# A two-layer block (selective scan, then experts): scan output and z kept with channels in rows

## The reference, cut to what matters

```python
z = zxbcdt[..., :D_INNER]
dt = softplus(zxbcdt[..., -H_SSM:] + dt_bias)
xBC = silu(causal convolution of 4 taps over the next 768 columns)
Y_diag = einsum('bcln,bcsn,bhcls,bcshp->bclhp', Cr, Br, Lmat, xdt)
Y_off = einsum('bcln,bchpn,bhcl->bclhp', Cr, states_prev, exp(Acs))
y = Y_diag + Y_off + D_param[None, None, :, None] * x_ssm
y = rmsnorm(y * silu(z), norm_gated_w)
out = y @ W_out.T + residual
```

## Time and profile before

| | |
|---|---|
| three executions, median (range) | 3193.36 us (3184.57 to 3193.8) |
| profiled execution, its own time | 3187.6 us |
| its span | 3185.9 us |
| TensorE clock granted, mean | 0.989 |
| busy: PE, PEld, DVE, ACT, POOL | 98%, 85%, 75%, 61%, 64% |

### The profile page before, as it was taken

How to read it: one execution, slowest core, us unless ns; L and a number is a source line. 1 busy time by engine, 2 the same in 40 slices (tenths; PEclk the granted TensorE clock), 3 DMA queues, 4 the chain that set the end, 5 groups by cost and what they waited for, 6 DMA issues and landing times.

```text
span 3185.9 us, 62383 instructions
## 1 busy us (share of the span) xinstructions
PE 3112.3 (98%) x19648; PEld 2722.1 (85%) x19648; DVE 2394.2 (75%) x5104; ACT 1935.2 (61%) x4149; POOL 2031.2 (64%) x2311
## 2 busy tenths in 40 slices
PE   5899999999999999999999999999999999999997
PEld 4688888888888888888888888888888888888886
DVE  5877877777777777777777777778777777777763
ACT  5565666665666556666566666656656656665562
POOL 2477666677666676656676666776666776666764
PEclk7899999999999999999999999999999999999999
DMA  3123222222222222222122222222222222222222
GB/s 123 41 68 87 73 73 67 66 66 85 73 64 64 71 73 76 80 66 58 64 86 76 76 60 66 66 86 73 73 66 66 66 86 73 64 67 69 73 74 48
DMA packets 143433, 227.33 MB, mean 71 GB/s; under 512 B 18976, under 2 KB 88352, under 8 KB 143392
## 3 DMA queue, kind: packets, MB, share of 16 engines
q1 hardware_dynamic: 126496, 210.06, 20.1%
q0 software_dynamic: 16896, 16.78, 4.0%
HBM read 174.87 MB, written 35.13 MB: 66 GB/s over the span
## 4 chain that ended last, share of the span: by engine, by line
PE 95%; DVE 0%; POOL 0%; ACT 0%; issue 0%; ACTq 0%; DVEq 0%; POOLq 0%
PE fpb L1443 34%; PE apb L1443 20%; PE acc L1629 17%; PE apb L1575 7%; PE apb L1452 4%; PE ppb L1443 3%; PE apb L1560 3%; PE apb L1567 2%; PE ppb L1462 2%; PE apb L1547 1%; PE fpb L1492 1%; PE fpb L1462 1%; PE fpb L1494 1%; PE fpb L1608 0%; PE apb L1520 0%; PE apb L1519 0%
## 5 line engine op out<-in xcount | busy, mean ns | idle before, releaser
L652 POOL TENSOR_TENSOR hidL<-hid,hidH 128x512 fp32r<-128x512 f32 x384 | 544.9, 1419 | 234.8 <-ACT hidH L914 226.8
L1130 DVE SCALAR_TENSOR_TENSOR xc<-apb,cw,xc 128x511 f32<-128x511 f32 (+2 forms) x576 | 427.8, 747 | 63.9 <-ACT xc L827 35.9
L1629 PE MATMUL acc<-WDH,hidH 128*128 128x256 f32 x1536 | 456.7, 297 | 4.4 <-POOLq L654 4.4
L914 ACT CAST hidH<-hid 128x512 fp32r<-128x512 f32 x384 | 236.2, 615 | 341.9 <-POOL hid L647 283.6
L1629 PE MATMUL acc<-WDH,hidL 128*128 128x256 f32 x1536 | 431.4, 281 | 0.0
L1629 PE MATMUL acc<-WDL,hidH 128*128 128x256 f32 x1536 | 430.9, 281 | 0.0
L647 POOL TENSOR_TENSOR hid<-hid,cb 128x512 f32<-128x512 f32 x256 | 347.5, 1358 | 73.2 <-DVEq L1251 42.1
L1249 DVE TENSOR_TENSOR hid<-hid,fpb 128x512 f32<-128x512 f32 x384 | 261.1, 680 | 135.6 <-PE fpb L1443 132.3
L1443 PE MATMUL fpb<-fTh,UH 128*128 128x512 f32 x768 | 335.7, 437 | 0.0
L845 ACT ACTIVATE seg<-seg,acs 128x128 f32<-128x128 f32 x1024 | 313.6, 389 | 11.5 <-ACT cb L895 5.7
L1443 PE MATMUL fpb<-fTh,GH 128*128 128x512 f32 x768 | 318.6, 415 | 0.0
(11 more groups left out here) (195 smaller groups left out, 8669.6 us busy)
## 6 DMA issues: line engine op xcount, KB each, us to landing
seg<-acs_row SPq DMA_DIRECT2D x128, 512.0 KB, 4.2
cb<-c_row SPq DMA_DIRECT2D x512, 128.0 KB, 2.9
xsP<-in_x SPq DMA_DIRECT2D x32, 512.0 KB, 3.6
xc<-qrot SPq DMA_DIRECT2D x32, 512.0 KB, 3.4
xc<-in_x SPq DMA_DIRECT2D x32, 512.0 KB, 4.3
out<-xc SPq DMA_DIRECT2D x32, 512.0 KB, 3.0
out<-xn POOLq DMA_DIRECT2D x32, 512.0 KB, 6.0
ZL_loaded<-in_wzx_t SPq DMA_DIRECT2D x2, 512.0 KB, 4.4
```

The costliest lines, as they stand in the source:

```text
L652: own.do(G.tensor_tensor(hidL[:, j % 2, :], hid[:, j % 2, :], hidH[:, j % 2, :].bitcast(fp32), ALU.subtract))
L914: A.copy(hidH[:, j % 2, :], hid[:, j % 2, :]).then_inc(sem["hidden_high"], 1)
L1130: ins = V.scalar_tensor_tensor(xc[:, b, s:], src[:, 0:T - s], cw[:, b, TAPS - 1 - s:TAPS - s], xc[:, b, s:], ALU.mult, ALU.add)
L1629: ins = nc.tensor.matmul(dst, l[:, w, tk], r[:, j, :], start=j == 0 and t % 2 == 0 and n == 0, stop=j == HB - 1 and n == 2, skip_group_che ...
```

## The change

The scan output and z are kept with channels in rows (128 channels x 512 tokens, four such blocks) from the matmul on.

- `project_z(j)` makes one block of z, 128 channels by 512 tokens, four per sequence. dt is computed apart by `project_dt`: 16 narrow matmuls (16 and 8 columns moving) into their own bank, read by `dt_bias_add` in two operations.
- `diagonal` swaps its operands: 64 columns of `xdt` are stationary and the 128 columns of `seg` move. Even heads write PSUM partitions 0 to 63, odd heads 64 to 127, so two heads lie side by side in the array's column halves.
- `from_state` becomes four matmuls with S stationary and C moving. The decay along the row that `state_part` needs is read from DRAM as rows (`own_rows` on SP, two DMAs) and exponentiated in one ACT operation over 128x1536 (`row_exp`) into `own_decay`, which shares its place with xTh and xTl.
- `times_dt` takes the D term from `xc` in SBUF, not from PSUM.
- `y_by_channel` is gone: `evac_y` and `y_low` read `zs` in SBUF.
- The sum of squares now goes over partitions: `square_y` writes the squares, `sum_squares` (DVE, two additions per chunk) folds four blocks to one, `squares_by_token` (PE) multiplies them by a column of ones, `squares_out` copies the result.
- yTh and yTl are guarded by `yT_read` and `out_begun` in place of PSUM slots; all step tables are written anew, in all stages.

```diff
+        own_decay = sb("own_decay", [P, (NT - 1) * NB, P])
...
+                    ("G3", "ACT", "ACT"), ("U2", "DVE", "DVE"), ("U3", "DVE", "DVE"), ("cT", "ACT", "ACT"),
+                    ("G4", "ACT", "ACT"), ("U4", "DVE", "DVE"), ("G5", "ACT", "ACT"), ("U5", "DVE", "DVE"),
...
+                sp.wait_ge(sem["acs_stored"], 16)
+                for a in range(2):
+                    sp.dma_start(own_decay[a * PD:(a + 1) * PD, :, :],
+                                 rows(acs_row, [[0, PD], [2 * P, (NT - 1) * NB], [1, P]], (HS + a) * P)
+                                 ).then_inc(sem["ear_loaded"], 16)
...
-                ins = G.tensor_tensor(zs[:, c, :], zs[:, c, :], xD[:, c % 2, :], ALU.mult)
+                gate = zs[:, :, c * P:(c + 1) * P]
+                ins = G.tensor_tensor(gate, gate, xD[:, c % 2, :].rearrange("p (j n) -> p j n", j=NB), ALU.mult)
...
+            def silu_z(j):
+                way.filled(act, "ACT", f"z{j}")
+                free("a", f"z{j}", A.activation(zs[:, j, :], way.bank(f"z{j}")[:], ACT.Silu))
+
+            def row_exp():
+                act.wait_ge(sem["ear_loaded"], 32)
+                A.activation(own_decay[:], own_decay[:], ACT.Exp).then_inc(sem["ear_ready"], 1)
...
             def evac_y(c):
-                way.filled(act, "ACT", f"yT{c}")
-                A.copy(yTh[:].rearrange("p j n -> p (j n)"), way.bank(f"yT{c}")[:]).then_inc(sem["yh_ready"], 1)
+                act.wait_ge(sem["yg_ready"], c + 1)
+
+                if c == 2:
+                    act.wait_ge(sem["out_begun"], 1)
+                elif c:
+                    act.wait_ge(sem["yT_read"], (c + 1) // 2)
+                A.copy(yTh[:], zs[:, :, c * P:(c + 1) * P]).then_inc(sem["yh_ready"], 1)
...
             def square_y(c):
+                act.wait_ge(sem["yg_ready"], c + 1)
                 if c >= 2:
-                    own.wait()
-                ins = A.activation(junk[c % 2], zs[:, c, :], ACT.Square, accum_out=ssy[:, c:c + 1])
-                if c % 2:
-                    ins.then_inc(sem["ssy_ready"], 1)
-                else:
-                    own.mark(ins)
+                    act.wait_ge(sem["sq_summed"], 1)
+                A.activation(junk[c % 2].rearrange("p (j n) -> p j n", j=NB), zs[:, :, c * P:(c + 1) * P], ACT.Square
...
-            def dt_bias_add(c):
-                way.filled(dve, "DVE", f"za{c}")
-                ins = V.tensor_tensor(dr[:, c, :], way.bank(f"za{c}")[:, DI // 2:DI // 2 + HS], dtb[:], ALU.add)
...
+            def dt_bias_add():
+                way.filled(dve, "DVE", "dt")
+                parts = way.bank("dt")[:, 0:2 * NT * HS].rearrange("p (t a h) -> p t a h", t=NT, a=2)
+                own.do(V.tensor_tensor(dr[:], parts[:, :, 0, :], dtb[:].unsqueeze(1).broadcast_to([P, NT, HS]), ALU.add))
+                own.do(V.tensor_tensor(dr[:], dr[:], parts[:, :, 1, :], ALU.add))
...
-                free("a", f"xt{c}", V.tensor_tensor(by_head(xD[:, c % 2, :]), by_head(way.bank(f"xt{c}")[:]),
-                                                    along(dbc[:]), ALU.mult))
+
+                ins = V.tensor_tensor(by_block(xD[:, c % 2, :]), xc[:, 0:NB, c * P:(c + 1) * P],
+                                      dcol[:].unsqueeze(2).broadcast_to([P, NB, P]), ALU.mult)
...
+            def own_part(c):
+                return own_decay[:, (c - 1) * NB:c * NB, :]
+
             def state_part(c):
                 way.filled(dve, "DVE", f"yo{c}")
-                own.do(V.tensor_tensor(by_head(ysp[:]), by_head(way.bank(f"yo{c}")[:]), along(ea[:, c, :]), ALU.mult))
+                if c == 1:
+                    dve.wait_ge(sem["ear_ready"], 1)
+                own.do(V.tensor_tensor(own_part(c), by_block(way.bank(f"yo{c}")[:]), own_part(c), ALU.mult))
                 free("a", f"yo{c}")
...
+                    ins = V.tensor_tensor(by_block(xdt[:, c % 2, :]), own_part(c), by_block(way.bank(f"yd{c}")[:]), ALU.add)
...
+                if c == 2:
+                    dve.sem_inc(sem["xT_free"], 1)
...
+            def out_begins():
+
+                dve.wait_ge(sem["out_ready"], 1)
+                dve.sem_inc(sem["out_begun"], 1)
...
             def y_low(c):
                 dve.wait_ge(sem["yh_ready"], c + 1)
-                free("a", f"yT{c}", V.tensor_tensor(yTl[:].rearrange("p j n -> p (j n)"), way.bank(f"yT{c}")[:],
-                                                    yTh[:].rearrange("p j n -> p (j n)").bitcast(fp32), ALU.subtract))
+                V.tensor_tensor(yTl[:], zs[:, :, c * P:(c + 1) * P], yTh[:].bitcast(fp32),
...
+            def sum_squares(c):
+
+                dve.wait_ge(sem["sq_ready"], c + 1)
+                q = junk[c % 2]
+                own.do(V.tensor_tensor(q[:, 0:2 * P], q[:, 0:2 * P], q[:, 2 * P:4 * P], ALU.add))
+                V.tensor_tensor(q[:, 0:P], q[:, 0:P], q[:, P:2 * P], ALU.add).then_inc(sem["qs_ready"], 1)
...
+            def squares_out(s):
+                way.filled(dve, "DVE", f"ss{s}")
+                own.do(V.tensor_copy(ssy[:, pair(s)], way.bank(f"ss{s}")[:, 0:2]))
+                free("a", f"ss{s}")
...
-            def project_z(c, n):
-
-                name, tk = f"z{'ab'[n]}{c}", slice(c * P, (c + 1) * P)
...
+            def project_dt():
+                b = slot("dt")
+
+                pe.wait_ge(s_hT, 2)
+                pe.sem_inc(s_hT, -2)
+                fill("dt", narrow(b, hTh, hTl, DTW, HS))
+
+            def project_z(j):
+
+                name, lo = f"z{j}", j * P + (HS if j >= NB // 2 else 0)
+                cs = slice(lo, lo + P)
...
                 read_out(f"st{c - 1}")
-                fill(f"yo{c}", nc.tensor.matmul(b[:], xc[:, 5, c * P:(c + 1) * P], S[:], start=True, stop=True))
+                for j in range(NB):
+                    js = slice(j * P, (j + 1) * P)
+                    ins = nc.tensor.matmul(b[:, js], S[:, js], xc[:, 5, c * P:(c + 1) * P], start=True, stop=True)
+                fill(f"yo{c}", ins)
 
...
-                    hs = slice(h * PD, (h + 1) * PD)
-                    ins = nc.tensor.matmul(b[:, hs], seg[:, c % 2, h, :], xdt[:, c % 2, hs], start=True, stop=True)
+
+                    half = slice(h % 2 * PD, (h % 2 + 1) * PD)
+                    ins = nc.tensor.matmul(b[half, h // 2 * P:(h // 2 + 1) * P], xdt[:, c % 2, h * PD:(h + 1) * PD],
+                                           seg[:, c % 2, h, :], start=True, stop=True)
                 fill(f"yd{c}", ins)
 
-            def y_by_channel(c):
-                b = slot(f"yT{c}")
-                pe.wait_ge(sem["yg_ready"], c + 1)
-                fill(f"yT{c}", transposes(b, lambda j: zs[:, c, j * P:(j + 1) * P], NB))
+            def squares_by_token(s):
+                b = slot(f"ss{s}")
+                for n in range(2):
+                    c = 2 * s + n
+                    pe.wait_ge(sem["qs_ready"], c + 1)
+                    ins = nc.tensor.matmul(b[:, n:n + 1], junk[n][:, 0:P], ones[:, 0:1], start=True, stop=True)
+                fill(f"ss{s}", ins)
...
                 b = way.bank(f"out{s}") if t % 2 else slot(f"out{s}")
-                read_out(f"yT{t}")
-                ins = split_mm(b[:, (t % 2) * D:(t % 2 + 1) * D], [(yTh[:, j, :], yTl[:, j, :], WOH[:, j, :], WOL[:, j, :])
-                                                                   for j in range(NB)])
+                pe.wait_ge(sem["yl_ready"], t + 1)
+                ins = split_mm(b[:, (t % 2) * D:(t % 2 + 1) * D],
+                               [(yTh[:, j, :], yTl[:, j, :], WOH[:, j, :], WOL[:, j, :]) for j in range(NB)])
...
+                h_by_channel(1); gate(11); settled("f_out_ACT"); settled("qn_ready"); up(11)
+                settled("f_out_DVE")
                 assert not open_
 
             def tail():
                 begin("tail", "afg")
...
```

More of the change, by code:

```diff
@@ L88, in build @@
         xdec = sb("xdec", [P, 2, DI])
[L89 removed]
+        xD = sb("xD", [P, 2, DI])
         seg = sb("seg", [P, 2, HS, P])
@@ L1054, in split_low @@
                 dve.wait_ge(s_high[n], 1)
-                for src, hi, lo, norm in SPLIT[n][1]:
+                for m, (src, hi, lo, norm) in enumerate(SPLIT[n][1]):
+                    if m:
+                        own.do(ins)
                     if norm is None:
@@ L1441, in split_mm @@
                 for ah, al, bh, bl in parts:
-                    for l, r in ((ah, bh), (ah, bl), (al, bh)):
+                    for l, r in ((ah, bh), (al, bh), (ah, bl)) if read is not None else ((ah, bh), (ah, bl), (al, bh)):
                         ins = nc.tensor.matmul(dst, l, r, start=n == 0, stop=n == total - 1)
@@ new lines, in iteration @@
+                gate(1); cumulate(); up(1); settled("ad_ready"); project_z(1); gate(2); project_x(3)
+                project_z(2); up(2); project_z(3); gate(3); CB(); B_by_token(); x_by_token(0); down(0)
+                settled("acc_free"); x_by_token(1); up(3); down(1); combine_by_expert(); down(2)
```

(17 more changed lines are left out.)

441 lines of the change are left out of this document (206 added, 235 removed).

## The result

The changed kernel takes 3366.83 us (median of 4 executions, 3363.69 to 3368.86), the kernel before, beside it, 3189.96 (4 executions, 3184.57 to 3193.8): ratio **1.0555 [1.0534, 1.0576]**, slower by 177 us or 5.7 us in each of the 31 passes. I had forecast 3164 and a range up to 3248. Both are wrong, and so is the sign.

What follows compares the result with a forecast made beforehand. TensorE, busy 98% of the span, was taken as the bound: -1.44 us of work and +0.5 of waits give -0.94 us per pass, times 31 = -29 us, so 3164 us; 8-in-10 range 3135 to 3248.

Steps and rivals of the forecast that it cites:

- term 7: Work off TensorE: VectorE rises from 73.9 to 80 to 86 us per pass; ScalarE, SP and POOL cost nothing.
- +0.5 of waits: TensorE's waits per pass, in us, around the output projections: 0.4 at squares_by_token(1), at worst 1.6; bounds 0 and 2.4.
- Everything else I checked: Other places where TensorE might wait, such as project_q(0) and project_out(1): each keeps about 1 us of slack.
- Rival A: VectorE falls behind at squares_by_token(1) and the output projections: 1.4 to 2.4 us of waits, 3192 to 3223 us; chance 0.15.
- Term 6: The diagonal: two column halves run together, 1.00 us plus 0.25 for switching array shape, against 1.73; -1.92 us per pass.
- Rivals B: At the diagonal the two column halves don't run together: +0.30 us per diagonal, 3245 us; chance 0.18.
- C: At the diagonal one half's loads don't hide behind the other's streams: +1.16 us per diagonal, 3352 us; chance 0.03.
- My estimate of 1.6x for two tiles: Alternative for the diagonal, from the skill's 2.38x for three column tiles: 1.1 us in place of 1.00.
- Terms 1 to 5: TensorE, us per pass: z -0.40, dt +1.68, y's transpositions -1.76, from_state +0.09, squares by ones +0.87.
- The sum without waits: TensorE's work per pass changes by -1.44 us, from a pass of 96.40 us.
- Rival D: The clock falls for one projection group after the pass's narrow matmuls and transpositions: +1.4 us per pass, 3208 us; chance 0.04.
- A's two parts: The split of the VectorE rival's 0.15 chance: 0.07 within 0.3% and 0.07 slower.

Runs made afterwards that it cites:

- number 1: The changed kernel with GpSimd's result_stored wait put back behind mask(1), all additions kept; 3270.01 us.
- number 2: The kernel before the change with only result_stored moved up right behind add_result(i - 2); 3267.01 us, ratio 1.024.
- number 12: number 10 with result_stored moved up again right behind add_result(i - 2), as in the changed kernel; 3270.06 us.
- number 3: The changed kernel without sum_squares' additions on VectorE, one block of four entering the sum, result_stored still early; 3277.76 us.
- number 4: The changed kernel with result_stored back behind mask(1) and sum_squares' additions left out; 3186.96 us, ratio 0.9994.
- number 10: number 1 with TensorE summing all squares, y_low(2) between norm_q(0) and mixed_out(0), and rest(8) ahead of norm_mixed(0); 3164.8 us.
- numbers 5: number 4 with y_low(2) moved ahead of norm_q(0) and mixed_out(0) on VectorE; 3251.64 us.
- 6: The changed kernel with result_stored behind mask(1), y_low(2) ahead of norm_q(0) and mixed_out(0), and all squares summed by TensorE; 3242.85 us.
- 8: number 1 with y_low(2) moved ahead of norm_q(0) and mixed_out(0), all additions kept; 3371.22 us.
- numbers 11: number 10 with the additions of sum_squares on VectorE again; 3301.04 us.

## Why the prediction was wrong

- **The failed step is in term 7: "SP and POOL do the same work but for two more row loads."** The work is the same, the order is not. I followed the new tables on PE and VectorE, and read GpSimd's for what it computes. Moving `result_stored` has a price of 97 us (number 1), 80 (number 2) and 105 (number 12), with no term in the sum and no place in the range. The kernel's text and the trace of the kernel before had what was needed: the diff of the two kernels shows the moved call, and the transfer took 6.0 us from issue to landing (median), for which a wait right behind the issue stands.
- **The second failed step is "Taken: +0.5 of waits, bounds 0 and 2.4".** VectorE's own waits are 3.6 us a pass (number 1). I priced one place, `squares_by_token(1)`, and there the upper bound of 1.6 held (1.2). "Everything else I checked (project_q(0) behind chunk_y(2), ...) keeps about 1 us" was false: `project_q(0)` waits 1.0, since `sum_squares(0)` now stands between `chunk_y(2)` and `x_low(0)` in the list (without the additions this wait is gone, number 3); and `project_out(2)`, which I had not looked at, waits 1.3 behind `norm_q(0)` and `mixed_out(0)`, and 1.6 even with the additions left out and GpSimd's wait put back (number 4). And the additions were mis-sized: 7.6 us per pass, not 3 to 6.
- Rival A named the engine, the place and the bound "from 1.44 us per pass on it eats the whole gain". It had 0.15 and ended at 3223; late_stored, which has A alone, stands at 3270. Bounds of waits taken from one place are no bounds for the list.
- **Term 6 was right**: 1.00 + 0.25 forecast, 1.02 and 1.58 - 1.40 = 0.18 behind it measured. In the inside it is a little otherwise than I had it: not nine steps of 0.111, but eight pairs that start together and step by 0.110 (0.16 for the first), and 0.21 until the projection. Rivals B and C are refuted. The Trainium skill (TensorEngine Tiling (Array Packing), Key Properties) says that a change of tiling mode drains the engine; the 0.18 fits that. My estimate of 1.6x for two tiles from the Trainium skill's figure for three (TensorE: Matmul & The Clock Gate, Measured speedup vs the span model) would have given 1.1; the rows say 1.73 / 1.02 = 1.7x against full width. The Trainium skill's sentence on loads that overlap only in another row group (TensorE: Matmul & The Clock Gate, The mechanism) is not borne out: sixteen records and their loads, all on the same rows, take 1.02.
- Terms 1 to 5: z 1.40 a block, dt 1.72 (forecast 1.68; 1551.42 to 1553.14 on the chain), `from_state` 0.89. Squares were 0.34 per two matmuls, 0.68 a pass, where I had 0.87. The sum without waits was 96.40 - 1.44 = 94.96; number 4 shows 94.6, number 10 shows 95.41 with 0.90 more for its squares, which is 94.5. That part of the sum was good to 0.5 us.
- Rival D (the clock) did not come from the narrow matmuls, as I had it. It comes behind waits, as in the pass shown above behind the one for `CBs`. It is a second price of a wait, small in the kernel after (once between 200 and 3100 us), larger in numbers 5, 6 and 8 (25, 22 and 29 times; the loop's clock 0.98, 0.99 and 0.97).
- The chances add up to 0.99, and A's two parts to 0.14 of its 0.15; nothing hangs on either.
- 3164.8 us for number 10 is my number to the microsecond, and no merit of mine: it is another kernel, with two lists put right and one sum on another engine.

## What to carry over

When a change rewrites order tables, price every wait that moves on every engine, also on those whose work is the same: read what stands behind it in that list, and follow that to the bound engine. A full engine fed by four in-order lists has no slack to be read as one number; a step that moves up pushes each step it passes, and the next list behind those. And work is not cheap because its engine has idle time: 7.6 us of additions in VectorE's list cost 136 us more than 0.9 us of them on the full engine (numbers 11 and 10), since the full engine stood behind that list.

## What I had not expected of the hardware

VectorE's operations on SBUF inputs are stretched by what GpSimd does at that moment, by about what is left of GpSimd's instruction. In number 10 the same `y_low`, twice within a few microseconds, on VectorE, and GpSimd's instructions beside it:

```profile
1532.82 0.69 DVE L1269 TENSOR_TENSOR yTl<-zs,yTh 128x512 fp32r<-128x512 f32 x1 [1.06 <-ACT yTh L890]
...
1538.60 1.78 DVE L1269 TENSOR_TENSOR yTl<-zs,yTh 128x512 fp32r<-128x512 f32 x1
```
```profile
1532.66 0.71 POOL L605 TENSOR_TENSOR ry<-ssy,mhalf 128x2 f32<-128x2 f32 x1
...
1538.49 1.34 POOL L665 TENSOR_TENSOR hid<-hid,cb 128x512 f32<-128x512 f32 x1
```

Beside an instruction of two columns it takes 0.69, beside one of 512 that began 0.11 earlier 1.78, and it ends 0.55 after that one. The Trainium skill (SBUF — State Buffer, SBUF: two separate sides) says that a VectorE operation with two SBUF inputs and a GpSimd one that reads SBUF exclude each other for a whole instruction. For GpSimd's instructions of 512 columns the trace agrees; the one of two columns is recorded with 0.71 us and did not hold `y_low` up. `x_low`, one of whose two inputs lies in PSUM, takes 0.66 to 0.69 us in all its 64 executions of this run, whatever GpSimd does. The additions of 128 columns in the kernel after take 0.29 us at the least and 1.36 at the most; those that start with more than 1.0 us of a GpSimd instruction left take 1.24 or more, all others 0.29. That is how their mean on `xdec` comes to 1.26. So where such an operation stands in time, and not its size, sets what it costs: `y_low` means 0.68 in the kernel after and 1.15 in number 10, which is the faster kernel. `norm_q`, one SBUF input, varies as well: 364 ns before, 827 after, on average.

The accumulating transfer that landed 6.0 us after its issue before (median) took 9.6 in the changed kernel. What made it longer was not tried. In the pass shown above the two loads of `seg`'s rows run beside it from its start (landed at 1580.37 and 1582.56 us), and before they had been issued 3 us ahead of it; the two new row loads are issued at 1582.28 and meet only its end.
